# A graph layer on one core: steps of 20 nodes for 16, and the step's small job moved ahead of the builds on the matmul engine

## The reference

```python
# x [12500, 128]; src, dst [400000], dst sorted; edge_type in {0, 1}
Xs = X[src]
m_data = Xs @ W_data.T + b_data
m_ctrl = Xs @ W_control.T + b_control
msg = where(edge_type == 0, m_data, m_ctrl)
agg = segment_sum(msg, dst, 12500)
y = X + relu(agg + (X @ W_self.T + b_self))
out = (y - mean(y)) / sqrt(var(y) + 1e-5)       # over the 128 features
```

## Time and profile before

| what | value |
|---|---|
| median of 3 runs | 2238.66 us (2237.98 to 2239.69) |
| profiled execution | 2245.35 us |
| its span, first to last instruction | 2243.6 us, 63546 instructions |
| mean granted TensorE clock | 0.978 of full speed |
| products L713 | 7840 matmuls, 1373.3 us busy |
| builds L694 | 12800 matmuls, 446.1 us busy |
| gathered sums L674 | 3080 matmuls, 212.4 us busy |
| gathers L609 on POOL | 1540, 1460.9 us busy |

### The profile page before, as it was taken

One profiled execution on the slowest core, in us unless ns is written; L12 is line 12 of the kernel. 1 busy time (PEld: TensorE's weight loads), 2 busy tenths in 40 slices (PEclk: granted clock), 3 DMA queues, 4 the chain that ended last, 5 costly groups with the idle time before them and its releaser, 6 DMA issues.

```text
span 2243.6 us, 63546 instructions
## 1 busy us (share of the span) xinstructions
PE 2109.6 (94%) x25270; PEld 1819.1 (81%) x25270; DVE 1542.3 (69%) x3920; ACT 1374.0 (61%) x2256; POOL 1511.6 (67%) x1602
## 2 busy tenths in 40 slices
PE   2789999999999999999999999999999999999997
PEld 1568888888888888888888888888888888888886
DVE  5777677676667667767767667667767766667673
ACT  2556666666656666656666666666666666566663
POOL 2767777577767567767767777666777766777750
PEclk9689999999999999999999999999999999999999
DMA  7332222122222122222212222212222212222210
GB/s 194 86 100 59 57 61 61 50 58 65 54 60 58 53 53 62 60 58 58 63 48 63 57 65 59 59 52 59 59 61 57 65 53 55 57 61 58 62 51 9
DMA packets 109995, 138.99 MB, mean 62 GB/s; under 512 B 39131, under 2 KB 83331, under 8 KB 109695
## 3 DMA queue, kind: packets, MB, share of 16 engines
q0 software_dynamic: 51680, 105.94, 18.0%
q1 hardware_dynamic: 45375, 22.55, 3.7%
q10 hardware_dynamic: 12640, 6.36, 1.1%
HBM read 125.35 MB, written 9.39 MB: 60 GB/s over the span
## 4 chain that ended last, share of the span: by engine, by line
PE 81%; DVE 8%; issue 3%; DVEq 2%; DMA 2%; POOL 2%; ACTq 1%; ACT 1%; POOLq 0%
PE apply_ps L713 49%; PE build L694 15%; PE sum_ps L674 8%; ACTq L861 1%; DVE hot_q L1159 1%; POOL rows L609 1%; DVEq L1203 1%; DVE acc L1212 1%; PE misc L738 1%; DVE hot_p L1156 1%; PE misc L768 1%; PE misc L755 1%; PE misc L766 1%; PE misc L722 1%; DMA out<-y_sb 1%
## 5 line engine op out<-in xcount | busy, mean ns | idle before, releaser
L609 POOL DMA_INDIRECT rows<-in_x,src_t x1540 | 1460.9, 949 | 645.8 <-issue 446.8
L887 ACT ACTIVATE cnt<-build 128x784 fp32r<-128x784 f32 x1520 | 1174.1, 822 | 714.5 <-PE build L694 651.0
L713 PE MATMUL apply_ps<-cnt,x 128*128 128x320 f32 x7840 | 1373.3, 321 | 7.3 <-issue 4.3
L713 PEld LDWEIGHTS apply_ps<-cnt,x 128*128 128x128 f32 x7840 | 1186.0, 192 | 55.6 <-issue 22.0
L1156 DVE TENSOR_TENSOR hot_p<-const_ps,key_pq 128x1024 bf16<-128x1024 bf16 x800 | 550.9, 689 | 423.2 <-PE build L694 406.2
L694 PEld LDWEIGHTS build<-hot_q,hot_p 64*128 64x128 bf16 x12800 | 321.5, 95 | 174.7 <-issue 139.9
L694 PE MATMUL build<-hot_q,hot_p 64*128 64x98 bf16 x12800 | 446.1, 208 | 15.6 <-DVE hot_q L1159 8.3
L1159 DVE TENSOR_TENSOR hot_q<-const_ps,key_pq 128x784 bf16<-128x784 bf16 x800 | 443.7, 555 | 0.0
L674 PE MATMUL sum_ps<-rows,hot 128*64 128x129 f32 x3080 | 212.4, 282 | 6.0 <-DMA rows<-in_x,src_t 6.0
L674 PEld LDWEIGHTS sum_ps<-rows,hot 128*64 128x64 f32 x3080 | 171.2, 138 | 22.5 <-DMA rows<-in_x,src_t 9.1
L1052 DVE TENSOR_TENSOR hot<-const_ps,key_t 128x640 f32<-128x640 bf16 x154 | 124.6, 809 | 16.0 <-ACT key_t L856 9.4
(11 more groups left out here) (179 smaller groups left out, 893.8 us busy)
## 6 DMA issues: line engine op xcount, KB each, us to landing
rows<-in_x,src_t POOLq DMA_INDIRECT x1540
x_raw<-in_x ACTq DMA_DIRECT2D x13, 448.0 KB, 9.5
key_dram<-x_u SPq DMA_DIRECT2D x18, 162.0 KB
x_u<-in_x SPq DMA_DIRECT2D x39, 64.0 KB
out<-y_sb SPq DMA_DIRECT2D x39, 64.0 KB
x_u<-in_x SPq DMA_DIRECT2D x36, 53.5 KB
out<-y_sb SPq DMA_DIRECT2D x36, 53.5 KB
win_i<-in_dst SPq DMA_DIRECT2D x25, 64.0 KB
```

What stands on the lines that cost most here:

```text
L609: pool.indirect_dma_start(out=rows[:, slot, 0:D], out_offset=None, in_=x, in_offset=bass.IndirectOffsetOnAxis(ap=src_t[:, col:col + 1], ax ...
L713: last = pe.matmul(sums, x2[:, b, D * k:D * k + D], counts(b - half * HALF, half), start=(b == 0 and k == 0), stop=(r == TURNS - 1 and hal ...
L887: act.activation(o, i.rearrange("p h (m b) -> p b h m", b=HALF), ACT.Copy).then_inc(evacuated, 1)
```

## The change

- **Steps of 20 nodes.** `NODES` is 20: 8 steps in a pass, 640 batches for 800, 648 steps for 810. One-hots come in 5 slots (`QUADS`). A pass's halves have 50 and 48 source blocks (`HALVES`) for 49 and 49; builds have 20 matmuls of 100 or 96 columns, evacuations and last moves 1000 or 960 columns, one-hots 1280 and 1000 or 960; a step has 12 products, two steps of the first half have 14. The numbers of products and of build matmuls stay.
- **Keys in groups of 240 nodes** (`KNODES`), 27 for 25; `prepare_keys` is called three steps ahead of the keys' job instead of one; the planner's distances are changed with it. Gather rounds fall on steps 3 and 7 of a pass.
- **Order on PE:** apply, job, build, gather sums.
- **Shapes of small matmuls:** `fin_deg` and `bias9` have 128 rows (the rest zero) for 9, in a ring that a unit never crosses; `zg` and `picks` share a tile, and the weights of L721 have 66 columns for 2.
- **Room:** the tiles of the end lie in `sg`, degree sums are kept per epoch instead of per unit, and the descriptor scratch of POOL's DMAs is 2048 for 4096.

```diff
-BLOCK = 64
-NODES = 16
+NODES = 20
+QUADS = NODES // 4
+KNODES = 240
+KTILES = KNODES // 4
+KBATCHES = KNODES // NODES
...
-DEG_RING = 3
+DEG_RING = 4
...
-    HALF = XBLOCKS // 2
-    SIDE = -(-HALF // TURNS) * TURNS
+    SIDE = XBLOCKS // 2 // TURNS * TURNS
+    HALVES = (XBLOCKS - SIDE, SIDE)
-    slots = [0] + [10 * p + o for p in range(PASSES) for o in (4, 9)][:-1]
+    slots = [0] + [TURNS * p + o for p in range(PASSES) for o in (3, 7)][:-1]
...
-        ptr_step[g] = place(6 if g == 1 else batch_of(g) - 27)
-        key_step[g] = place(batch_of(g) - 6)
+        ptr_step[g] = place(6 if g == 1 else max(batch_of(g) - 22, key_step[g - 1] + 4))
+        key_step[g] = place(batch_of(g) - 5)
...
-    key_round = {min(r for r in range(PAIRS) if gather_step[r] >= s + (8 if g == 1 else 14)): g
+    key_round = {min(r for r in range(PAIRS) if gather_step[r] >= s + (6 if g == 1 else 11)): g
...
-                s = 4 * (n % 2)
+                s, H = QUADS * (n % 2), HALVES[n // TURNS % 2]
...
-                    for j in range(4 * z, 4 * z + 4):
+                    for j in range(QUADS * z, QUADS * z + QUADS):
...
-                            o = WIDE * h + 2 * HALF * (j % 4)
-                            last = pe.matmul(build_ps[z][:, o:o + 2 * HALF], hot_p[part, s + pair, :, r],
-                                             hot_q[part, s + pair, :, r], start=True, stop=True)
+                            o = WIDE * h + 2 * H * (j % QUADS)
+                            last = pe.matmul(build_ps[z][:, o:o + 2 * H], hot_p[part, s + pair, :, r],
+                                             hot_q[part, s + pair, 0:2 * H, r], start=True, stop=True)
...
-                pe.matmul(misc[0:2, P:P + 64], zg[:, :], picks[:, :], start=True, stop=True)
+                pe.matmul(misc[0:66, P:P + 64], zg_picks[:, :], picks, start=True, stop=True)
...
-                ring = DEG_RING * 4 * BLOCK
-                a = v.n0 % ring
-                if a + v.r <= ring:
-                    return pe.matmul(o, fin_deg[:, a:a + v.r], bias9[:, :], start=False, stop=True)
-                k = ring - a
-                pe.matmul(o[0:k, :], fin_deg[:, a:ring], bias9[:, :], start=False, stop=True)
-                return pe.matmul(o[k:v.r, :], fin_deg[:, 0:v.r - k], bias9[:, :], start=False, stop=True)
+                a = v.n0 % (DEG_RING * KNODES)
+                return pe.matmul(o, fin_deg[:, a:a + v.r], bias9[:, :], start=False, stop=True)
...
-                if batch_at(s) is not None:
-                    build(batch_at(s))
-                if s in gather_at:
-                    gather_sums(gather_at[s])
                 if s in job:
                     pe.wait_ge(misc_free, job[s])
                 if keys_at(s) is not None:
...
                     turn_x(turn_at[s])
                 if s in out_at:
                     unit_out(out_at[s])
+                if batch_at(s) is not None:
+                    build(batch_at(s))
+                if s in gather_at:
+                    gather_sums(gather_at[s])
...
-        bias9 = sb("bias9", [9, D], BF16)
+        bias9 = sb("bias9", [P, D], BF16)
-        fin_deg = sb("fin_deg", [9, DEG_RING * 4 * BLOCK], BF16)
+        fin_deg = sb("fin_deg", [P, DEG_RING * KNODES], BF16)
...
-                    hot_p[:, s:s + 4, :, :], table_p.unsqueeze(1).to_broadcast([P, 4, P, 2]),
-                    keys_p.unsqueeze(2).to_broadcast([P, 4, P, 2]), ALU.is_equal)
+                    hot_p[:, s:s + QUADS, :, :], table_p.unsqueeze(1).to_broadcast([P, QUADS, P, 2]),
+                    keys_p.unsqueeze(2).to_broadcast([P, QUADS, P, 2]), ALU.is_equal)
                 dve.tensor_tensor(
-                    hot_q[:, s:s + 4, :, :],
-                    table_q[:, half, :, :].unsqueeze(1).to_broadcast([P, 4, 2 * HALF, 2]),
-                    keys_q.unsqueeze(2).to_broadcast([P, 4, 2 * HALF, 2]), ALU.is_equal).then_inc(onehot_ready, 1)
+                    hot_q[:, s:s + QUADS, 0:2 * H, :],
+                    table_q[half].unsqueeze(1).to_broadcast([P, QUADS, 2 * H, 2]),
+                    keys_q.unsqueeze(2).to_broadcast([P, QUADS, 2 * H, 2]), ALU.is_equal).then_inc(onehot_ready, 1)
...
-                if keys_at(s + 1) is not None:
-                    prepare_keys(keys_at(s + 1))
+                if keys_at(s + 3) is not None:
+                    prepare_keys(keys_at(s + 3))
...
-    nc = bacc.Bacc("TRN2", target_bir_lowering=False, num_devices=1, dynamic_dma_scratch_size=4096)
+    nc = bacc.Bacc("TRN2", target_bir_lowering=False, num_devices=1, dynamic_dma_scratch_size=2048)
```

More of the change, by code:

```diff
@@ L126, in gnn_resnorm @@
     UNITS = len(units)
+    last_of = {(v.n0 - WIN_0) // EPOCH_NODES: i for i, v in enumerate(units) if not v.dense}
+    epoch_of = {i: e for e, i in last_of.items()}
+    assert sorted(last_of) == list(range(EPOCHS - 1))
     turn_at = {v.turn: i for i, v in enumerate(units)}
@@ L169, in dense_rows @@
     def dense_rows(r, half):
-        return range(r, HALF, TURNS) if half else range(SIDE // TURNS * r, min(HALF, SIDE // TURNS * (r + 1)))
+        if half:
+            return list(range(r, SIDE, TURNS))
+        k, more = SIDE // TURNS, HALVES[0] - SIDE
+        return list(range(k * r, k * r + k)) + [SIDE + i for i in range(more) if r == TURNS - more + i]
     job, jobs = {}, 2
@@ L232, in gnn_resnorm @@
         t_mask = sb("t_mask", [P, 2])
-        picks = sb("picks", [P, 64], F16)
+        zg_picks = sb("zg_picks", [P, 2 + 64], F16)
         low = sb("low", [P, 2])
@@ L273, in gnn_resnorm @@
         x2f = x2[:, :, :].bitcast(F32)
[L274 removed]
+        turned = cnt[:, 0:SIDE * COLS].rearrange("p (j c) -> p j c", j=TURNS)
         def counts(q, half):
@@ L701, in apply @@
                 G, half = divmod(t, 2)
-                blocks = [half * HALF + q for q in dense_rows(r, half)]
+                blocks = [half * HALVES[0] + q for q in dense_rows(r, half)]
                 if r == 0:
@@ L712, in apply @@
                     for k in range(2):
-                        last = pe.matmul(sums, x2[:, b, D * k:D * k + D], counts(b - half * HALF, half),
+                        last = pe.matmul(sums, x2[:, b, D * k:D * k + D], counts(b - half * HALVES[0], half),
                                          start=(b == 0 and k == 0), stop=(r == TURNS - 1 and half == 1
@@ L1146, in make_onehots @@
+                dve.tensor_tensor(deg_ok[:, :], deg_ok[:, :], deg_new[:, :], ALU.add)
             def make_onehots(n):
                 nb = TURNS * (n // (2 * TURNS)) + n % TURNS
-                half, s = n // TURNS % 2, 4 * (n % 2)
-                g, q = nb // 16, 8 * (nb % 16)
+                half, s = n // TURNS % 2, QUADS * (n % 2)
+                H = HALVES[half]
+                g, q = nb // KBATCHES, 2 * QUADS * (nb % KBATCHES)
                 if n >= 2:
                     dve.wait_ge(built, 2 * (n - 1))
-                if half == 0 and nb % 16 == 0:
+                if half == 0 and nb % KBATCHES == 0:
@@ L1252, in take_out @@
                 dve.sem_inc(misc_free, 1)
-                if not v.dense:
-                    dve.tensor_reduce(deg_sum[:, i:i + 1], acc_deg[0:2, v.buf, v.c0:v.c0 + v.r], AX.X, ALU.add)
+                if i in epoch_of:
+                    e = epoch_of[i]
+                    skip = max(DENSE - WIN_0 - EPOCH_NODES * e, 0)
+                    dve.tensor_reduce(deg_sum[:, e:e + 1], acc_deg[0:2, e % 2, skip:EPOCH_NODES], AX.X, ALU.add)
                 moments(i, v.r)
@@ L1304, in _ @@
             dve.wait_ge(misc_free, JOBS)
-            for j, v in enumerate(ends):
-                if not v.dense:
-                    last = dve.tensor_reduce(deg_sum[:, UNITS + j:UNITS + j + 1],
-                                             acc_deg[0:2, v.buf, v.c0:v.c0 + v.r], AX.X, ALU.add)
-            step(last)
+            dve.memset(end_mv, 1.0)
+            e, rest = EPOCHS - 1, N - WIN_0 - EPOCH_NODES * (EPOCHS - 1)
+            step(dve.tensor_reduce(deg_sum[:, e:e + 1], acc_deg[0:2, e % 2, 0:rest], AX.X, ALU.add))
             dve.tensor_reduce(deg_all[:, 2:3], deg_ok[:, :], AX.X, ALU.add)
```

133 lines of the change are left out of this document (73 added, 60 removed).

## The result

The changed kernel takes 2226.6 us (median; 2224.7 to 2227.7) against 2238.6 (2238.0 to 2239.7) before: a ratio of 0.9945, with a 95% interval from 0.9928 to 0.9962, or 12 us less. The forecast was 10 less. The profiled execution took 2227.7 us, its span is 2225.6.

What follows compares the result with a forecast made beforehand. Bound: PE's stream, per-step fixed costs and hand-overs of PSUM bank `misc`. -46 - 8 - 47 + 53 + 9 + 9 + 4 + 16 = -10 from profiled 2245.35 gives 2235.4; median lies 6.7 lower, 2228.7 us; 8-in-10 range 2196 to 2262.

Steps and rivals of the forecast that it cites:

- Alternations, -46: PE's switches between products and builds: 160 fewer, each step saved worth 0.29 us, -46 us.
- Degree matmul, -8, and columns, 0: Small PE matmuls: full-height degree matmul saves 0.14 us in 58 dense outputs, -8 us; 66-column weights 0, bounded by +-8.
- Keys, -47: PE's key waits: preparing two steps earlier removes 38.8 us and about half of 17 us for late `hot_q`, -47 us.
- Sums job followed by a job, +53: PE's wait for bank `misc` behind VectorE: 85 waits of 0.78 us for 67 of 0.2, +53 us.
- Turns and pointers, +9 and +4: Bank hand-overs to a following job: 92 turns of x at 0.1 us, +9; 14 pointer jobs at 0.3, +4.
- Late VectorE in last steps, +9: Sums job behind an output job in a pass's last step, 22 times: VectorE about 0.4 us late, +9 us.
- Pass boundary, +16: Products at a pass's end wait for VectorE's wider last move: 75 times 0.22 us, +16 us.
- The first 140 us, 0: Start of the kernel: paced by dense keys' round trips and gathers, not PE's counts; 0, +-8 us.
- the first (waits of 1.1 to 1.3 us): Rival: VectorE late in most sums steps, 85 waits of 1.1 to 1.3 us; 2256 to 2273 us; chance 0.25.
- The second (a job cheaper between products and build): Rival: PE's switches get cheaper, 434 jobs save 0.05 to 0.1 us each; 2186 to 2207 us; chance 0.2.
- The gathers: Rival: GpSimd's gathers become the bound locally, +5 to +20 us; 2234 to 2249 us; chance 0.06.
- The rate of the Trainium skill: Rival: VectorE one-hots at one element a cycle, each of 85 waits 0.23 us longer; 2248 us; chance 0.01.

Runs made afterwards that it cites:

- E8: Changed kernel with VectorE and ScalarE emptying the bank before one-hots and evacuations, a pass's last move still ahead of VectorE's bank work: 2148.4 us (0.9596).
- E1: Changed kernel with PE's old order, build and gathered sums before the job again: 2123.8 us (0.9483).
- E3: Changed kernel, new order kept, with keys prepared one step ahead of their job instead of three: 2283.9 us (1.0202).
- E10: Changed kernel with PE's old order and keys prepared one step ahead instead of three: 2112.8 us (0.9432).
- E6: Kernel before, with the two addresses of a sums job read ahead of the last move and one-hots on VectorE: 2224.5 us (0.9932).

## Why the prediction was right, and where its steps were not

The sum hit (-10 forecast, -12 measured) and its mechanism held: work and key waits go, waits for the bank come in front of a build. That it hit so closely is luck in part. Two things that the sum had at nothing went opposite ways: what a job between products and build costs PE beside the waits (24.6 us, E8 against E1), and the clock, which falls around the long waits for keys (some 22 us in the profiled execution, some 10 between the medians, both estimates).

- **Alternations, -46: right.** Twelve products take 1.97 us as forecast, a build 0.55 in the mean of both widths for 0.57. A step without job and gather has a median of 2.14 us before and 2.53 after; four of the new for five of the old, less the two products that these have more (0.29), save 0.29 us, 160 times: 47 us.
- **Degree matmul, -8, and columns, 0.** Some -10 and, as run, -8 in the old order. I had bounded the columns by +-8 and took the middle; the measured value is the bound. Nothing in the trace of before could tell that narrow weights cost more between products and build than between build and products: 0.2 against 0.09 us. In the new order the tall shapes save 34, and are part of what makes it bearable.
- **Keys, -47: right for the changed kernel, and too small by the clock.** E3 gives 46.6 us of key waits back when the two steps are taken away, and PE's weight loads wait 15.9 us for `hot_q` where they waited 32.1. What I missed is the second cause: in the old order the planner, which puts nearly every key job beside a gather, removes the waits by itself (E10). My note that key jobs "cost no hand-over" in gather steps was half of this. The two steps more pay for the new order (57 us, E3) and cost some 7 at the start (E1 against E10), within the +-8 that I allowed.
- **Sums job followed by a job, +53: right as a difference, both sides off.** Bank free at 2.97, not 3.21; PE there at 2.41 (E8), not 2.54. I scaled the wider one-hots onto an interval that contained 0.28 us of waiting for addresses; that pause absorbed the width, as E6 bears out. The cost in the median step is 0.74 us where 0.78 was forecast. At 85 x 0.74 = 63 us of cost, less the 13 for the waits of before, it is 50.
- **Turns and pointers, +9 and +4: low.** 14 and 7.5 us, in the table. **Late VectorE in last steps, +9:** hardly seen: 0.79 us in the median of the 21 outside the start, where the others have 0.72, under 2 us.
- **Pass boundary, +16: right,** 2.04 us from the build's start to the products, where build and gathered sums alone would take 1.81 (0.56 and 1.25): 0.23 us, though my own figures (2.08 less 1.83) gave 0.25. It comes of the wider move, as the old order's kernel has it too without a job. What the order adds there is that the job is no longer beside the move: 12 us, a step that I had missed.
- **The first 140 us, 0: fine for the sum.** 9 us of the order's price fall into the first 60 steps.

Of the rivals, the first (waits of 1.1 to 1.3 us) did not come in steps of 20; in steps of 16 the hand-over costs 0.86. The second (a job cheaper between products and build) is refuted: E8, without the waits, is 24.6 us slower than the old order. Keys were there in time except once. The gathers did not bind the changed kernel, but do share the bound once the order's cost is gone (E1). The rate of the Trainium skill (VectorE: DVE Perf Modes, "The perf-mode tier table") for a PSUM operand is not what this chip does with `const_ps`: 1280 elements take 822 ns and 1024 took 689, 0.52 ns each.

```profile
L1174 DVE TENSOR_TENSOR hot_p<-const_ps,key_pq 128x1280 bf16<-128x1280 bf16 x640 | 526.3, 822 | 435.7 <-PE build L707 428.0
```

I had put 0.33 on slower, because waits of 0.78 and 0.95 us are close. That doubt was fair, but it was aimed at the size of one term. What the prediction didn't ask is what the change would be worth without its order: -115 or, with the keys left one step ahead, -126. E10, at 2112.8 us, is the fastest of all these kernels.

## What to carry to other kernels

A job that waits for a shared buffer must stand on the bounding engine where other work covers the wait; moved ahead of a build, it puts the consumers' whole queue into every step. If it is moved, move the readers' places in their own queues as well (78 of the 103 us came back so), but not ahead of what the next products wait for. Where PE stands long for something, look at the granted clock behind the wait before pricing it. And take a bundle apart: here one part cost 103 us in a change that gained 12, and another was needed only because of it.

## What the runs showed that I had not expected

- A long wait of PE costs more than itself. Of the eleven waits for keys of 1.6 us or more that the kernel before has behind its first 180 us, ten go with a stretch of 3.4 or 6.8 us at 1.2 GHz; without these waits (the changed kernel, E10) there is no such stretch, and with them back (E3) there are ten.
- Two columns of weights in place of 66 cost 0.2 us per job when the matmul stands between products and a build, and 0.09 between a build and products.
- With two register loads of addresses on VectorE, the first instruction that uses them starts, in the median, 1.45 us after the start of the one-hots ahead: behind 1.17 us of one-hots this is a pause of 0.28 us, behind 1.39 us one of 0.05. Loading them earlier gained 14 us in one kernel and lost 10 in another.
- Gathers on GpSimd kept their 948 ns and 0.30 us between them with half the descriptor scratch (949 ns in the earlier trace rows).
